# Graph attention multiplies h2's rows ahead of its weight; score terms as row sums on VectorE, softmax sums on ScalarE, probabilities divided on GpSimd

## The reference, cut to what matters

```python
# layer 0, h: (b, n, 256), 8 heads of 32
attn = jnp.einsum('bhnd,bhmd->bhnm', q, k) * scale
attn = jnp.where(attn_mask[None, None] == 0, -jnp.inf, attn)
attn = jax.nn.softmax(attn, axis=-1)
o = jnp.einsum('bhnm,bhmd->bhnd', attn, v)...            # then w_proj, bias, o + layernorm(o)
# layer 2, graph attention
h = jnp.einsum('bnc,cf->bnf', x, W)
s1, s2 = h @ a[:F_, 0], h @ a[F_:, 0]
e = jax.nn.leaky_relu(s1[:, :, None] + s2[:, None, :], negative_slope=0.2)
att = jax.nn.softmax(e * mask[None, :, :], axis=2)
return jax.nn.elu(jnp.einsum('bij,bjf->bif', att, h) + beta * h)
```

## Time and profile before

| | |
|---|---|
| median of three runs | 1475.9 us (1473.24 to 1476.55) |
| the profiled execution: its own time, its span | 1474.63 us, 1472.8 us |
| TensorE matmul busy | 1438.2 us, 98% of the span, 16136 matmuls |
| TensorE weight loads busy | 1370.3 us, 93% |
| VectorE busy | 1273.4 us, 86%, 5774 instructions |
| ScalarE busy | 1134.7 us, 77%, 2884 instructions |
| GpSimd busy | 748.4 us, 51%, 1107 instructions |
| DMA | 39.90 MB, the x and result queue 7.9% of the 16 engines |
| TensorE's mean granted clock | 0.995 of full |

### The profile page before, as it was taken

How to read it: one execution, slowest core, us unless ns; L and a number is a source line. 1 busy time by engine, 2 the same in 40 slices (tenths; PEclk the granted TensorE clock), 3 DMA queues, 4 the chain that set the end, 5 groups by cost and what they waited for, 6 DMA issues and landing times.

```text
span 1472.8 us, 47814 instructions
## 1 busy us (share of the span) xinstructions
PE 1438.2 (98%) x16136; PEld 1370.3 (93%) x16136; DVE 1273.4 (86%) x5774; ACT 1134.7 (77%) x2884; POOL 748.4 (51%) x1107
## 2 busy tenths in 40 slices
PE   5999999999999999999999999999999999999996
PEld 5899999999999999999999999999999999999985
DVE  4889988988989889889889889889889889889885
ACT  4778878878877877877877778778778788788753
POOL 3455555555555555555555555555555555555452
PEclk9999999999999999999999999999999999999998
DMA  3000000100000000001001000000001001000000
GB/s 111 17 17 23 31 16 30 31 16 31 30 17 31 30 16 31 28 19 31 24 23 30 23 24 30 24 24 31 23 24 30 23 24 30 19 28 31 9 23 30
DMA packets 38113, 39.90 MB, mean 27 GB/s; under 512 B 2416, under 2 KB 37488, under 8 KB 37872
## 3 DMA queue, kind: packets, MB, share of 16 engines
q1 hardware_dynamic: 37872, 36.84, 7.9%
HBM read 20.05 MB, written 16.78 MB: 25 GB/s over the span
## 4 chain that ended last, share of the span: by engine, by line
PE 95%; DVE 1%; ACT 1%; issue 1%; POOL 0%; DMA 0%; SPq 0%; POOLq 0%; ACTq 0%; DVEq 0%
PE bank L314 34%; PE mid L314 15%; PE bank L349 6%; PE mid L358 5%; PE bank L520 5%; PE bank L370 4%; PE mid L458 4%; PE mid L374 4%; PE bank L330 4%; PE mid L488 4%; PE bank L417 4%; PE mid L330 2%; PE mid L349 2%; PE mid L493 1%; PE mid L527 1%
## 5 line engine op out<-in xcount | busy, mean ns | idle before, releaser
L546 ACT ACTIVATE probs<-masked,neg_max 128x128 f32<-128x128 f32 x1024 | 326.3, 395 | 6.3 <-DVE neg_max L716 6.3
L903 POOL TENSOR_TENSOR rstd<-var_eps,minus_half 128x2 f32<-128x2 f32 x320 | 240.9, 753 | 25.5
L716 DVE CUSTOM_DVE_ANT_0 masked<-mid,mask 128x128 f32<-128x128 f32 x1024 | 234.9, 286 | 6.9 <-issue 6.8
L915 POOL TENSOR_TENSOR xb<-x,b_proj_beta 128x512 f32<-128x512 f32 x64 | 81.9, 1279 | 233.9 <-DVE o_res L828 233.9
L901 POOL TENSOR_TENSOR var_eps<-mean_var,eps 128x2 f32<-128x2 f32 x320 | 63.5, 198 | 243.0 <-DVE mean_var L710 242.7
L706 DVE BATCH_NORM_STATS2 stats<-x 128x6 f32<-128x256 f32 x384 | 143.3, 415 | 0.1
L725 DVE TENSOR_SCALAR z<-x,mean_var,rstd 128x256 f32<-128x256 f32 x384 | 134.5, 405 | 7.1 <-POOL rstd L903 6.7
L946 POOL TENSOR_TENSOR h_t_lo<-h_t_full,h_t_hi 128x512 fp32r<-128x512 f32 x64 | 82.0, 1282 | 79.4 <-ACT h_t_hi L629 79.4
L349 PE MATMUL bank<-ident,probs 128*128 128x128 f32 x768 | 117.6, 276 | 4.9 <-ACT probs L546 4.9
L942 POOL TENSOR_TENSOR e_mask<-e_leaky,adj_sb 128x256 f32<-128x256 f32 x64 | 46.8, 731 | 116.2 <-DVE e_leaky L770 116.2
L370 PE MATMUL bank<-probs_t,v 128*32 128x128 f32 x2048 | 104.5, 276 | 0.3 <-issue 0.3
(11 more groups left out here) (156 smaller groups left out, 5725.8 us busy)
## 6 DMA issues: line engine op xcount, KB each, us to landing
x<-in_x SPq DMA_DIRECT2D x64, 256.0 KB, 2.7
out_x<-x SPq DMA_DIRECT2D x64, 256.0 KB, 2.1
w_qkv_sb<-in_w_qkv SPq DMA_DIRECT2D x1, 768.0 KB, 4.4
w_q_sb<-in_w_q SPq DMA_DIRECT2D x1, 256.0 KB, 4.4
w_k_sb<-in_w_k SPq DMA_DIRECT2D x1, 256.0 KB, 4.6
w_v_sb<-in_w_v_t SPq DMA_DIRECT2D x1, 256.0 KB, 5.8
w_proj_sb<-in_w_proj SPq DMA_DIRECT2D x1, 256.0 KB, 6.0
w_gat_x<-in_w_gat SPq DMA_DIRECT2D x1, 256.0 KB, 7.2
```

Of the source, the lines that this page charges most:

```text
L546: last = act.activation(probs[:, r, s], masked[:, r, s], ACT.Exp, scale=-1.0, bias=neg_max[:, r, s:s + 1])
L716: last = dve.tensor_tensor_reduce(out=masked[:, r, s], in0=mid[:, r, s * N:(s + 1) * N], in1=mask[:], scale=1.0, scalar=LARGE, op0=ALU.add ...
L903: pool.tensor_tensor(rstd[:, k], var_eps[:, k], minus_half[:], ALU.pow).then_inc(ln_rstd[k], 1)
```

## The change

- `heads_times_values` loses the 16 matmuls with ones. Each exponential gets `accum_out`, so ScalarE delivers the row sums as it writes the probabilities; VectorE takes their reciprocals, eight at a time; GpSimd multiplies the probabilities with them in place, one instruction of 128 x 512 for each group of four, ahead of the transposes. ln and exp(-x) are gone, and the heads' high part comes from the bank on ScalarE, the low part from the bank on VectorE (it was GpSimd's).
- Graph attention: h2 = relu(norm(x2)) is made by ScalarE as rows and isn't transposed. s1 and s2 are row sums of h2 times (w_gat a), four `tensor_tensor_reduce` of 256 columns on VectorE per pair; the rows w_gat a are spread once, in the set-up. s1 plus s2 and the leaky relu are one Prelu on ScalarE. m = (att h2) transposed is an fp32 product, split into high and low part, and then multiplied with w_gat (12 matmuls of 256 columns) into u.
- z of layers 0 and 1 is made by ScalarE with scale and bias (`shift`), where VectorE's `normalize` made it.
- All is spread over ten streams, 73 steps; the order of the parts on each engine, and the banks, are new. w_qkv is split in thirds, and w_q and w_k are loaded after the constants of layer 0 and folded in step 2.

The diff's core:

```diff
-    STREAMS = 8
+    STREAMS = 10
...
-                            pe.matmul(heads_bank[at, to], v0[:, b, hc * RG + r], probs_t[:, r, s],
-                                      start=True, stop=True, tile_position=(0, r * HD))
-                        for r in range(RG):
-                            at = slice(r * HD, (r + 1) * HD)
-                            last = pe.matmul(sums_bank[at, to], ones[:], probs_t[:, r, s],
+                            last = pe.matmul(heads_bank[at, to], v0[:, b, hc * RG + r], probs_t[:, r, s],
                                              start=True, stop=True, tile_position=(0, r * HD))
...
+                    pe.wait_ge(s12_ready, done(p6))
+                    bank_free(pe, (max_ready[2], p2, 1), (x4_ready, p10, 1), (v0_ready, p3, 1))
+                    for b in range(2):
+                        last = pe.transpose(s2_bank[:, b * N:(b + 1) * N], s12[:, b, 1:2].to_broadcast([128, 128]), ident[:])
+                    last.then_inc(s2_psum, 1)
...
-                    for b in range(2):
-                        last = pe.matmul(u_bank[:, b * D:(b + 1) * D], att_t[:, b], hw[:, b, 0:D], start=True, stop=True)
-                    last.then_inc(u_psum, 1)
...
-                    bank_free(pe, (v1_ready, p3, 1), (g_ready, p3, 1), (h_hi_ready[1], p3, 1))
-                    bank_free(pe, (h_lo_ready[2], p4, 1), (max_ready[2], p1, 1), (q_ready, p1, 1))
-                    rows([hw0_bank[:, 0:DX], hw1_bank[:, 0:DX]], h_t[2], w_gat_p, 0, DX).then_inc(hw_psum, 1)
...
+                    pe.wait_ge(att_t_ready, done(p6))
+                    pe.wait_ge(h2_ready, done(p6))
+                    bank_free(pe, (x3_ready, p7, 1))
+                    for c in range(C):
+                        for b in range(2):
+                            last = pe.matmul(m_bank[:, (c * 2 + b) * N:(c * 2 + b + 1) * N], h2[:, b, c * 128:(c + 1) * 128],
+                                             att_t[:, b], start=True, stop=True)
+                    last.then_inc(m_psum, 1)
...
+                    pe.wait_ge(v0_ready, done(p2))
+                    bank_free(pe, (probs_t_ready[0], p2, 1), (q_ready, p1, 1), (o_ready, p3, 1))
+                    heads_times_values().then_inc(heads_psum, 1)
...
+                    bank_free(pe, (m_lo_ready, p6, 1))
+                    rows(halves(u_bank), m_t_p, w_gat_p, 0, D).then_inc(u_psum, 1)
...
                     last = act.activation(probs[:, r, s], masked[:, r, s], ACT.Exp, scale=-1.0,
-                                          bias=neg_max[:, r, s:s + 1])
+                                          bias=neg_max[:, r, s:s + 1], accum_out=sums[:, r, s:s + 1])
                 return last
...
+                    act.wait_ge(s2_psum, done(p6))
+                    wait_before(act, e_mask_ready, p6)
+                    for b in range(2):
+                        act.activation(e_leaky[:, b], s2_bank[:, b * N:(b + 1) * N], ACT.Prelu, bias=s12[:, b, 0:1], alpha=ALPHA)\
+                           .then_inc(e_leaky_ready, 1)
...
-                if on[2]:
-                    act.wait_ge(heads_psum, done(p2))
-                    act.activation(ln_sum[:], sums_bank, ACT.Ln).then_inc(ln_sum_ready, 1)
-                    act.wait_ge(ln_sum_ready, done(p2))
-                    wait_before(act, o_norm_ready, p2)
-                    act.activation(inv_sum[:], ln_sum[:], ACT.Exp, scale=-1.0).then_inc(inv_sum_ready, 1)
...
+                    act.wait_ge(m_psum, done(p6))
+                    wait_before(act, u_psum, p6)
+                    act.activation(flat(m_t_p[0]), m_bank, ACT.Copy).then_inc(m_hi_ready, 1)
+                if on[5]:
+                    act.wait_ge(shift_ready[2], done(p5))
+                    wait_before(act, m_psum, p5)
+                    for b in range(2):
+                        last = act.activation(h2[:, b], x2[:, i5, b], ACT.Relu, bias=shift[2][:, b:b + 1], scale=rstd[:, 2, b:b + 1])
+                    last.then_inc(h2_ready, 1)
...
+                    wait_before(act, h_t_psum[0], p0)
+                    for b in range(2):
+                        last = act.activation(z[0][:, b], x0[:, i0, b], ACT.Identity, bias=shift[0][:, b:b + 1],
+                                              scale=rstd[:, 0, b:b + 1])
+                    last.then_inc(z_ready[0], 1)
...
+                    dve.tensor_tensor(flat(m_t_p[1]), m_bank, flat(m_t_p[0]).bitcast(f32), ALU.subtract).then_inc(m_lo_ready, 1)
...
+                    wait_before(dve, e_leaky_ready, p5, 2)
+                    dve.memset(s12_turn[:], 0.0)
+                    for b in range(2):
+                        for j in range(2):
+                            last = dve.tensor_tensor_reduce(out=s12_prod[:, b, j], in0=h2[:, b], in1=wa_rows[:, j], scale=1.0, scalar=0.0,
+                                                            op0=ALU.mult, op1=ALU.add, accum_out=s12[:, b, j:j + 1])
+                    last.then_inc(s12_ready, 1)
+                if on[2]:
+                    dve.wait_ge(o_hi_ready, done(p2))
+                    dve.tensor_tensor(o_t_p[1][:].rearrange("p b c n -> p (b c n)"), heads_bank,
+                                      o_t_p[0][:].rearrange("p b c n -> p (b c n)").bitcast(f32), ALU.subtract).then_inc(o_lo_ready, 1)
...
+                if on[2]:
+                    dve.wait_ge(probs_ready[0], done(p2))
+                    dve.wait_ge(probs_ready[1], done(p2))
+                    dve.reciprocal(inv_sums[:, 0:2], sums[:, 0:2]).then_inc(inv_sums_ready[0], 1)
...
+                    pool.wait_ge(inv_sums_ready[0], done(p2))
+                    pool.tensor_tensor(probs[:, 1], probs[:, 1], inv_sums[:, 1].unsqueeze(2).to_broadcast([128, BC, N]), ALU.mult)\
+                        .then_inc(probs_norm_ready[1], 1)
```

More of the change, by code:

```diff
@@ L99, in gnn_stack @@
         rstd = sb("rstd", [128, NORMS, 2])
+        shift = [sb(f"shift{k}", [128, 2]) for k in range(3)]
         shift3 = sb("shift3", [128, 2])
         z = [sb(f"z{k}", [128, 2, D]) for k in range(3)]
[L102 removed]
+        h_t = [parts(f"h_t{k}", [128, C, 2 * N]) for k in range(2)]
         h_t1_full = sb("h_t1_full", [128, C, 2 * N])
@@ new lines, in step @@
+                if on[1]:
+                    act.wait_ge(q_psum, done(p1))
+                    wait_before(act, scores_psum, p1)
+                    act.activation(flat(q_t), q_bank, ACT.Copy, scale=-SCALE).then_inc(q_ready, 1)
+                if on[4]:
+                    act.wait_ge(shift_ready[1], done(p4))
+                    wait_before(act, h_t_psum[1], p4)
+                    for b in range(2):
+                        last = act.activation(z[1][:, b], x1[:, i4, b], ACT.Identity, bias=shift[1][:, b:b + 1],
+                                              scale=rstd[:, 1, b:b + 1])
+                    last.then_inc(z_ready[1], 1)
@@ L670, in _ @@
+            run(act, step, [(0, first_weights), (3, copy_fold), (3, copy_wa_rows)])
         @block.vector
@@ new lines, in step @@
+                if on[6]:
+                    dve.wait_ge(att_ready, done(p6, 2))
+                    dve.reciprocal(att_inv[:], att_sum[:]).then_inc(att_inv_ready, 1)
+                    dve.wait_ge(att_inv_ready, done(p6))
+                    wait_before(dve, att_t_psum, p6)
+                    for b in range(2):
+                        dve.scalar_tensor_tensor(att_norm[:, b], att[:, b], att_inv[:, b:b + 1], beta_ident[:],
+                                                 ALU.mult, ALU.add).then_inc(att_norm_ready, 1)
```

791 lines of the change are left out of this document (398 added, 393 removed).

## The result

| | before | after |
|---|---|---|
| median of four runs, us | 1474.76 (1473.24 to 1476.55) | 1578.65 (1577.34 to 1579.11) |
| profiled execution: own time, span, us | 1474.6, 1472.8 | 1579.1, 1577.3 |
| one step in mid-run, us | 22.20 | 23.76 |

The changed kernel is slower by 7.0%: ratio 1.070, 95% interval 1.068 to 1.072. The forecast was 4% faster. 64 steps of 23.76 leave 56.7 of the span for the ends, where the forecast had 55, so the whole miss is 2.5 us in every step.

The account below looks back on a forecast made before the run. TensorE was taken to set the pace before and after: 64 steps of 21.26 us plus 55 us for the ends gave 1415.6, stated as 1416 us, 4% under 1475.9, with a range of 1392 to 1452.

Parts of the forecast that it names:

- Do the hand-overs fit?: Layout of one step with TensorE gapless; every tight place between engines kept some slack, 0.5 to 1.6 us.
- v1's copy before rel_v: Tight place on ScalarE behind all sixteen exponentials: 0.9 us spare, late if an exponential costs 0.06 more than 0.40.
- a hand-over decides: Rival: a tight place fails by 0.3 to 0.8 us a step through a longer latency; 1437 to 1470 us, chance 0.13.
- The rival of VectorE and GpSimd slowing each other: Row sums beside GpSimd's divisions take twice their 1.4 us; step 21.7, 1445 us, chance 0.08.
- five tiny instructions, +0.5: Item in VectorE's sum per step: five new tiny instructions add 0.5 us.
- VectorE's term, 19.3: VectorE's work per step: 19.7 us before the change, 19.3 after removals and additions.
- The reason against: On GpSimd, o_t_lo shares its time with VectorE yet varies only from 1274 to 1303 ns in 64 executions.
- rstd's 1076 ns: On GpSimd, two-column rstd takes 688 ns at best, 1076 at worst, with VectorE busy beside it; cited for contention.
- My price for it: On VectorE, contention was priced as row sums taking twice their 1.4 us, giving 20.7 us of work.
- TensorE's sum: TensorE's step loses 0.94 us, from 22.20 to 21.26 (21.0 to 21.6 by the bounds).
- The term of the order: On TensorE, six blocks of products instead of four follow an fp32 group: +0.2 us, taken as 0 with counter-effects.
- ScalarE ends last: Rival: accumulator reads fail to overlap the next exponential, at most 0.2 us each; step 23.3, 1548 us; slower 0.09, mostly this.

Follow-up runs that it names:

- The second buffer: The changed kernel with a second pair of buffers for h_t0's two parts, alternating by pair: 1515.8 us against 1578.7 for the changed kernel.
- the last kernel: The kernel with both edits, with VectorE reordered: x's moments stand before the first att_norm, x2 between the two: 1394.9 us, ratio 0.9452 against the kernel before.
- the kernel with both edits: The changed kernel with second buffers for h_t0 and the four shifts made on GpSimd: 1418.6 us, ratio 0.9606 against the kernel before.
- the first probe kernel: The kernel before plus four two-column VectorE instructions ahead of o (reciprocal, PSUM sum, product with row sum, scalar_tensor_tensor): 1479.8 us against 1472.3.
- the second: The kernel before plus two two-column VectorE instructions ahead of o, a tensor_scalar and a tensor_tensor of two SBUF operands: 1477.6 us.

## Where the prediction was wrong

**"Do the hand-overs fit?" is the step that failed, twice.**

*A wait was missing from the layout.* My list had bank hand-overs and products, and not that h_t0's high part waits for v0's product of the pair before. ScalarE reaches this part 2.35 us before that product is over, and the code (L614) makes it stand there. The prediction did name v1's copy before rel_v as tight (0.9 spare), and it is v1 that is late, but not because an exponential costs more than 0.40: they start 0.38 to 0.39 apart. From the heads' copy (1017.37) to the end of v1's (1029.49) it is 12.1 us, 2.36 of them this wait; the other 9.8 are even less than the 10.1 forecast. The second buffer by itself gives back 63 us. The rival "a hand-over decides" was right in kind; its 0.3 to 0.8 us per step was too small, since it took a latency to be what fails and not a position in a queue. The wait holds eleven instructions behind it.

*The rival of VectorE and GpSimd slowing each other was set aside on the wrong row.* It was given the row sums, at 1.4 us more. The row sums run 0.34 to 0.35 apart in the changed kernel, because GpSimd is idle there (1016.8 to 1022.1). What paid were the shifts, in the sum among "five tiny instructions, +0.5", and att_norm, not in the sum at all for it was there before. VectorE's term, 19.3, came out at 22.1. Without the holding it was good: the last kernel, with the four shifts gone from VectorE, has 19.0 (80.13 of 88 us, a step of 20.82). The reason against, o_t_lo's 1274 to 1303 ns, says nothing: o_t_lo ran beside instructions that pass (bn_stats of 1016.33). The row that spoke for it, rstd's 1076 ns, was right. A row sum is held too when GpSimd is at work: with the shifts on GpSimd it meets x3b.

```profile
L864 DVE CUSTOM_DVE_ANT_0 s_prod<-h,wa_rows 128x256 f32<-128x256 f32 x256 | 129.7, 559 | 1.0 <-issue 1.0
```

The rule that I cited then, the contention in the Trainium skill (GPSIMD Engine Reference, the table of specifications), agrees with these runs for two SBUF inputs. My price for it, twice the row sums' time, was the error: what is paid is the rest of GpSimd's running instruction, and a 0.14 us instruction took 0.94.

**TensorE's sum**: 21.26 forecast, 20.82 measured (bounds 21.0 to 21.6, so it lies outside). The removed pieces and m are right to 0.1 (m takes 0.90, forecast 0.99). The term of the order was wrong in sign. I counted +0.2 for products that follow an fp32 group, and start to start the eight blocks of products do take 0.2 more in the last kernel than before. But the group ahead of them is then shorter, which I put at nothing: rel_v followed by k's products takes 0.68 (1006.79 to 1007.47 in the last kernel), followed by the scores it took 0.96 before (1013.28 to 1014.24). This group alone gives back more than the 0.2.

**ScalarE**: the accumulator's read overlaps the next exponential, 0.385 from start to start, so the rival "ScalarE ends last" did not happen. That the kernel came out slower, as this rival alone had said, is luck for it: its cause was not the one. **GpSimd**: a division takes 1.03 to 1.09, not 1.30. **Ends**: 56.7, forecast 55. None of these mattered.

That the forecast 1416 lies near the 1418.6 of the kernel with both edits is partly luck: there a TensorE step overestimated by 0.44 met a VectorE that still costs 0.34 by held instructions, and that kernel isn't the one that was forecast.

## What to carry to other kernels

In a software pipeline with fixed queues, list for every instruction that changes place each wait that it carries, those that protect a single buffer too, and then ask what is queued behind it: a ready instruction behind a waiting one is as late as the wait. Close every such chain once around the step; its length is a lower bound of the step beside each engine's sum. Where VectorE and GpSimd both work from SBUF, look at what each long GpSimd instruction runs beside, instruction by instruction; put PSUM reads, bn_stats or reductions there, and the tiny SBUF ones at its end.

## What the runs showed of the hardware

- A VectorE instruction of the forms scalar_tensor_tensor and product with row sum with two SBUF tensors, or tensor_scalar with one, that starts beside a running GpSimd instruction gets on only when that one is over, whatever its size. Two columns took 0.14 to 0.15 us alone, and 0.54, 0.68, 0.82 and 0.94 us held. A longer one then still has its own work to do: the att_norm pair of 2.24 us (128 columns each) ended 0.14 behind the second division, the first row sum beside x3b (256 columns) 0.28 behind it (1013.75 + 1.03 against 1013.21 + 1.29), x_exp (512 columns) 0.55 behind the division beside it (1000.95 + 0.78 against 1000.14 + 1.04). Reciprocal, reduction, bn_stats, a copy from PSUM and sums with one PSUM operand were not held.
- It seems to go the other way too, though no run was made for it. With both edits GpSimd's two-column var_eps took 0.61 us (1001.18 to 1001.79) beside VectorE's x_exp (until 1001.73), where it takes 0.19 to 0.20 with VectorE at bn_stats, and rstd 0.89 instead of 0.69 beside o_gam:

```profile
1001.18 0.61 POOL L951 TENSOR_TENSOR var_eps<-mean_var,eps 128x2 f32<-128x2 f32 x1
1001.87 0.89 POOL L953 TENSOR_TENSOR rstd<-var_eps,minus_half 128x2 f32<-128x2 f32 x1
```

- Between two GpSimd instructions that follow each other at once, a waiting VectorE instruction gets in: the last one of the first probe kernel took 0.15 just as x3b started, and x3b took its usual 1.30. The tensor_tensor of the second took 146 to 150 ns there in all 64 executions.
- A GpSimd product of 128x512 with a broadcast operand took 1.03 to 1.09 us, the sum of two full tensors 1.27 to 1.30.
